# Carried counts of a tile sort added by ten small products instead of one vector product, and a rank layout turned, in a graph transformer on Trainium2

## What is computed

```python
xn = layernorm(x, ln1_g[l], ln1_b[l])
deg = segment_sum(ones, src)            # normalised over the nodes
xp = xn + (xn @ Wpos[l] + bpos[l] + deg[:, None] * Wdeg[l][0] + bdeg[l])
q, k, v = heads(xp @ Wq[l] + bq[l]), heads(xp @ Wk[l] + bk[l]), heads(xp @ Wv[l] + bv[l])
att = clip(einsum('ehd,ehd->eh', q[dst], k[src]) / scale, -50, 50)
ex = exp(att - segment_max(att, dst)[dst])
aggr = segment_sum(v[src] * (ex / segment_sum(ex, dst)[dst]), dst)
x = x + (aggr @ Wo[l] + bo[l])
x = x + (gelu(layernorm(x, ln2_g[l], ln2_b[l]) @ W1[l] + b1[l]) @ W2[l] + b2[l])
```

## Time and profile before

| | us |
|---|---|
| median of three runs | 3694.4 |
| lowest and highest run | 3688.84, 3702.03 |
| profiled execution | 3699.51 |
| its span | 3697.7 |

### The profile page before, as it was taken

One profiled execution on the slowest core, in us unless ns is written; L12 is line 12 of the kernel. 1 busy time (PEld: TensorE's weight loads), 2 busy tenths in 40 slices (PEclk: granted clock), 3 DMA queues, 4 the chain that ended last, 5 costly groups with the idle time before them and its releaser, 6 DMA issues.

```text
span 3697.7 us, 72970 instructions
## 1 busy us (share of the span) xinstructions
PE 2986.3 (81%) x24671; PEld 2336.4 (63%) x24671; DVE 2910.8 (79%) x6776; ACT 1763.5 (48%) x4391; POOL 2521.1 (68%) x2601
## 2 busy tenths in 40 slices
PE   4783678788888888888877688888888888888887
PEld 4562466666766666666655466666766666666665
DVE  9886678787788888888876487877778787777775
ACT  1331235454545454554554345555456555555554
POOL 5006777777677777777775577777767777777773
PEclk6795679998999899999998689999899999999996
DMA  3005445555555555555553455555455565555552
GB/s 96 14 25 177 119 133 165 153 167 152 149 168 154 163 155 156 166 163 156 169 157 105 117 161 167 172 173 168 142 168 166 170 179 166 169 176 167 167 168 75
DMA packets 404552, 548.31 MB, mean 148 GB/s; under 512 B 78345, under 2 KB 318650, under 8 KB 403982
## 3 DMA queue, kind: packets, MB, share of 16 engines
q0 software_dynamic: 123648, 337.81, 31.3%
q1 hardware_dynamic: 273024, 198.55, 17.9%
q10 hardware_dynamic: 7506, 7.20, 0.6%
HBM read 518.00 MB, written 25.29 MB: 147 GB/s over the span
## 4 chain that ended last, share of the span: by engine, by line
PE 43%; DVE 21%; ACT 11%; POOL 10%; issue 8%; DMA 5%; SPq 1%; DVEq 1%; ACTq 0%; POOLq 0%
PE psum L937 9%; POOL kv_ring L1951 7%; PE psum L1027 5%; PE psum L994 4%; PE psum L978 4%; DVE att L1655 4%; DMA arena<-sorted_table 3%; DVE work L1358 3%; PE psum L1011 2%; POOL arena L1951 2%; DVE scratch L1646 2%; PE psum L955 2%; ACT arena L1219 2%; PE psum L815 2%; ACT scratch L1208 2%
## 5 line engine op out<-in xcount | busy, mean ns | idle before, releaser
L1951 POOL DMA_INDIRECT kv_ring<-kv_table,src_idx x1936 | 1854.8, 958 | 709.0 <-issue 580.4
L1208 ACT ACTIVATE scratch<-psum 128x512 f32<-128x512 f32 x1148 | 646.7, 570 | 596.7 <-PE psum L947 374.3
L1951 POOL DMA_INDIRECT arena<-kv_table,src_idx x640 | 612.7, 957 | 202.8 <-issue 192.6
L937 PE MATMUL psum<-arena 128*128 128x256 f32 x1764 | 505.4, 409 | 64.6 <-ACT arena L1219 60.8
L1655 DVE TENSOR_REDUCE att<-scratch 128x64 f32<-128x1024 f32 (+1 forms) x448 | 524.8, 1171 | 0.1
L978 PE MATMUL psum<-q_win,scratch 64*128 64x128 f32 x5152 | 419.0, 308 | 98.4 <-DVE scratch L1646 61.5
L978 PEld LDWEIGHTS psum<-q_win,scratch 64*128 64x128 f32 x5152 | 353.9, 208 | 209.4 <-issue 165.2
L1219 ACT COPY arena<-psum 128x512 f32<-128x512 f32 x504 | 263.4, 532 | 443.6 <-PE psum L937 434.5
L1646 DVE TENSOR_TENSOR scratch<-psum,kv_ring 128x512 f32<-128x512 f32 x484 | 310.5, 683 | 156.0 <-DMA kv_ring<-kv_table,src_idx 116.8
L994 PE MATMUL psum<-scratch 128*64 128x136 f32 x5152 | 419.2, 311 | 13.1 <-ACT work L1307 8.0
L937 PEld LDWEIGHTS psum<-arena 128*128 128x128 f32 x1764 | 311.1, 197 | 170.7 <-ACT arena L1219 117.1
(11 more groups left out here) (253 smaller groups left out, 4739.2 us busy)
## 6 DMA issues: line engine op xcount, KB each, us to landing
arena<-kv_table SPq DMA_DIRECT2D x126, 896.0 KB
kv_ring<-kv_table,src_idx POOLq DMA_INDIRECT x1936
q_win<-q_table SPq DMA_DIRECT2D x644, 32.0 KB
work<-kv_table SPq DMA_DIRECT2D x98, 128.0 KB
arena<-kv_table,src_idx POOLq DMA_INDIRECT x640
q_win<-q_table SPq DMA_DIRECT2D x126, 64.0 KB
work<-q_table SPq DMA_DIRECT2D x98, 64.0 KB
kv_table<-work SPq DMA_DIRECT2D x49, 128.0 KB
```

Source lines behind the costliest of these rows:

```text
L937: mm = e.matmul(to[:, t % 2 * 2 * D:(t % 2 + 1) * 2 * D], hot_source[:, t * P:(t + 1) * P], source_rows[:, t, :], start=True, stop=True)
L1208: e.activation(to[:, at:at + width], apart[k % 2][:, 0:width], ACT.Relu, bias=1.0, scale=-1.0).then_inc(apart_read, 1)
L1951: e.indirect_dma_start(kv[m % RING_KV][:, t, :], None, kv_table[l], bass.IndirectOffsetOnAxis(ap=src_idx[:, c * T + t:c * T + t + 1], axis ...
```

## The change

In the rank steps, `s_carry` and `sort_carry` go. PE first makes the same product of `before` and `s_oh`, and then ten products of 49 columns each, one per edge tile of the run: the stationary operand is one column of `earlier` (40 values), repeated 128 times with step 0, the moving operand is `s_tot` [40, 49], and the results go to every tenth of the 490 columns, beginning at column t. They accumulate onto the first product; the last one signals. The rank step now waits for the totals only, and `sort_total` counts one per sort. `s_sel` is laid out with the ten edge tiles outside and the 49 source tiles inside: the multiplication writes it at steps of 49 values (98 bytes), and the reduction reads 49 values that lie side by side.

```diff
-        *s_carry, s_sel = (part_of(RUNS * NT // 2).bitcast(BF16).rearrange("p (b g) -> p b g", g=RUNS) for _ in range(3))
+        s_sel = part_of(RUNS * NT // 2).bitcast(BF16).rearrange("p (g b) -> p g b", g=RUNS)
...
-                    e.wait_ge(sort_total, (SA + 1) * j + 1)
+                    e.wait_ge(sort_total, j + 1)
...
-                e.wait_ge(sort_total, (SA + 1) * s + q + 2)
+                e.wait_ge(sort_total, s + 1)
                 flat = ps[:, 0:NT * RUNS]
+                by_tile = flat.rearrange("p (b g) -> p g b", g=RUNS)
                 e.matmul(flat, before[:], s_oh[:, q].rearrange("p b g -> p (b g)"), start=True, stop=False)
-                e.matmul(flat, ones_b[0:ST, :], s_carry[q % 2][0:ST].rearrange("p b g -> p (b g)"), start=False, stop=True
-                         ).then_inc(sort_ranked, 1)
+
+                for t in range(RUNS):
+                    n = q * RUNS + t
+                    mm = e.matmul(by_tile[:, t], earlier[0:ST, n:n + 1].to_broadcast([ST, P]), s_tot[0:ST], start=False,
+                                  stop=t == RUNS - 1)
+                mm.then_inc(sort_ranked, 1)
...
-            elif k == 5:
-                sort_carry(e, s, 0)
...
-                if k == 7 + 3 * q and q + 1 < SA:
-                    sort_carry(e, s, q + 1)
-                elif k == 8 + 3 * q and q < SA:
+                if k == 8 + 3 * q and q < SA:
...
-                    e.tensor_reduce(whole, s_sel.rearrange("p b g -> p g b"), AX_X, ALU.add).then_inc(sort_picked, 1)
+                    e.tensor_reduce(whole, s_sel, AX_X, ALU.add).then_inc(sort_picked, 1)
...
-                    e.tensor_tensor(s_sel.rearrange("p b g -> p (b g)"), ps[:, 0:NT * RUNS],
-                                    s_oh[:, q].rearrange("p b g -> p (b g)"), ALU.mult).then_inc(sort_picked, 1)
+                    e.tensor_tensor(s_sel.rearrange("p g b -> p b g"), ps[:, 0:NT * RUNS].rearrange("p (b g) -> p b g", g=RUNS),
+                                    s_oh[:, q], ALU.mult).then_inc(sort_picked, 1)
...
-        def sort_carry(e, s, q):
-
-            e.wait_ge(sort_total, (SA + 1) * s + 1)
-            e.tensor_tensor(s_carry[q % 2][0:ST], by_run(earlier[0:ST])[:, q].unsqueeze(1).to_broadcast([ST, NT, RUNS]),
-                            s_tot[0:ST].unsqueeze(2).to_broadcast([ST, NT, RUNS]), ALU.mult).then_inc(sort_total, 1)
```

## The result

The changed kernel takes 3719.3 us in the median (3712.3 to 3733.2, 8 runs) against 3697.7 us for the kernel before (3685.4 to 3709.3, 8 runs): **1.0071 times as long, 95% interval 1.0054 to 1.0088**. It is slower by 21.5 us, where I had forecast 3 us less and a range that ended at 3713 (both from the three runs known then, median 3694.4). The profiled execution took 3716.8 us (span 3715.1), 17.3 us more than that of before.

What follows compares the result with a forecast made beforehand. POOL's gather stream was taken to set the pace, PE and DVE costing time only where they hold it up. Terms -5.0 + 8.7 - 5.0 + 0 - 2 = -3.3 us gave 3691 against the median 3694.4; range 3673 to 3713.

Steps and rivals of the forecast that it cites:

- my terms for the carry, the ten products and POOL: Chain time: carry product removed from DVE -5.0 us, ten small PE products +8.7, POOL's own pace -2.
- L1042's row: PE row of forty 49-column products, moving operand at steps of 20 bytes; its 0.09 us was taken per small product.
- the L955 row: PE row of four 128-column products, each loading 128 weights: 0.08 us each, or 0.05 without the 0.11 us.
- my second rival: Slower (15%): stepped PSUM writes pace each small PE product at 0.25 us, giving +19 us, 3713.
- The reduction: DVE sum of chosen ranks (L1742), reading side by side: 1022 ns down to 0.60 us, -5.0 us on the chain.
- the term that I had set to 0: DVE picking product (L1763), 657 ns: unchanged by its stepped write, or at most 1.02 us, +3.4 us on the chain.
- the seven sorts: Seven sorts of ten (28 runs of 40) where time off the PE and DVE chain shortens the end.
- Sort seven: A sort where POOL was held only 0.3 us, since the ring of four chunks absorbed it.
- my signs: Trace checks: POOL's waits 52 to 62 us (above 70: PE underestimated), picking product 0.66 or near 1.0, products 0.06 to 0.12 apart.
- The third: The new layout does nothing (13%): the multiplication's stepped write loses what the reduction wins, 3694.5 us.
- The first: Faster (22%): DVE is what is late in the sorts and its relief passes in full, -21 us, 3673.

Runs made afterwards that it cites:

- the fifth chip: The one follow-up chip that ran the kernel before in about 3698 us; on the other four it took 5585 to 5649 us.
- the products alone: Ten small products and no carry, chosen ranks laid out as in the kernel before: ratios 1.0000, 1.0007, 1.0016 on slower chips, 3692.6 against 3698.0 us (0.9983) elsewhere.

## Why the prediction was wrong

**What held.** POOL's gathers set the pace and the change counted only through POOL's waits: 29.4 us more waits and 8.4 us less of POOL's own time account for the result. The carry was not measured alone. Its removal together with the ten products gives -5.3 us on the fifth chip (interval -14 to +2), where my terms for the carry, the ten products and POOL give -5.0 + 8.7 - 2 = +1.7. The ten products were mis-sized: 0.043 us apart where I took 0.09 from L1042's row. With that 14 x (10 x 0.043 + 0.11) - 5.4 = +2.2, and the three terms give -4.8. The row that was nearest in columns misled me; the L955 row (0.05) was the better one. L1042's moving operand lies at a step and that of the new products does not, which may be why, but no run takes them apart. The stepped write in PSUM, my second rival's ground, does not keep the products from following each other closer than those of L955. The reduction: 656 ns, forecast 600.

**What failed** is the term that I had set to 0: "*The product that picks the ranks now writes at steps of 98 bytes.*" I bounded it from above by the pace of the stepped read, 2.1 ns a value and 1.02 us, and the trace after shows 4.9 ns and 2.41 us. A read was taken as the bound of a write. The bound would have held for 4-byte values (0.98 us), and nothing that I read in the trace of before was a 2-byte write at steps. Put into my own sum with the pieces counted there, 13 on the chain, it costs 13 x 1.75 = +22.8 us. The reduction's term becomes -4.4 (12.2 us, 36% shorter), and the whole sum is -5.0 + 2.2 - 4.4 + 22.8 - 2 = +13.6 us, against +21.5 in the medians and +17.3 in the profiled pair. The fifth chip says where the remainder lies: the products alone fit my terms (-5.3 against -4.8), the layout does not (+24.5 against 22.8 - 4.4 = +18.4). A likely reason, not shown by itself, is that more DVE work brings more of it onto the chain: of the 28 runs in the seven sorts 16 picking products are on it now, where 13 were, and of all 40 it is 20, with 46.9 us, where 15 were. The first and the last of these pieces in the chain (start us, us, engine and line):

```profile
489.89 2.32 DVE arena L1764
...
2675.84 2.33 DVE arena L1764
```

Sort seven, which the ring had absorbed, began to hold POOL, as I had said of the second rival, but for another reason. Of my signs, POOL's waits at 90.6 us, above 70, said rightly that the loss reached POOL, but I had put that down to PE beforehand, and it was DVE. The product at 2.41 us lay outside both values that I had allowed, and the ten products at 0.043 us below their 0.06 to 0.12.

The rule of the Trainium skill that I quoted for this place (Advanced Engine Details and Errata, section Memory Cachelines) did point to it: an access that changes its line each time pays a penalty. For this write the trace agrees. The section gives no size, and between a read and a 2-byte write the size differs by 1.4 us in 490 values. Its rule for PSUM, that a non-contiguous pattern slows matmuls, does not show here: products of 49 columns with results at steps of 40 bytes start 0.043 us apart. No run has the same products with flat results to set beside them.

**The rivals.** The third, that the write loses what the reduction wins, was the right mechanism with a bound too low; the write lost 1.75 us for the reduction's 0.37. The second ended on the right side, and near the time, by luck: its reason, slow products, is refuted by the products alone. The first fell: DVE got more work, not less.

## What to carry to other kernels

Where a layout is turned so that a reduction reads side by side, look at who writes it: on DVE a product with 2-byte values written at steps took 3.7 times as long as with the flat write, with 4-byte ones 1.5 times, and a read at steps 1.6 times. When a cost isn't in the trace, bound it by a row of the same direction and width, or say that there is none and widen the range. And where one queue keeps an exact pace, sum the others' work only where they hold it up, but let the sum grow when a buffer that absorbed it runs full.

## What the runs showed of the hardware

- DVE, 128 partitions, 490 values, output at steps of 98 or 128 bytes in bf16: 2407 and 2344 ns; at 196 bytes in f32: 981 ns; flat: 657 ns. The next instruction starts 2.00 us after the 2-byte stepped write and 0.58 us after the flat one, and it can be slowed as well: 1.46 in place of 1.21 us for the messages, 0.88 in place of 0.65 us for the carry product.
- A stationary operand of one column repeated 128 times with step 0, with 49 moving columns and results ten words apart in PSUM, costs 0.043 us per product with its own weight load at the full granted clock, 0.078 us at the lower one.
- POOL's 2576 gathers took 2467.5 us in the trace of before, 2459.4 in the trace after and 2463.4 with the products alone on the fifth chip. Both of the latter lack the forty carry products, so 4.1 to 8.1 us less come with their removal, where I had given it 2. That it is the cause isn't shown: three traces of the products alone on other chips differ by 8 us among themselves.
- The kernel before took 3698 us in the first comparison and on the fifth chip, and 5585 to 5649 us on the four others. The traces from those four, of changed kernels, show equal durations of single DVE instructions; the engines stood waiting for products of TensorE that completed late. What delays them was not found.
